# K and V of a cross attention in five matrix products instead of six, with a doubled half of the channels

## The reference, cut to what matters

```python
q = (query @ Wq + bq)                # 100 x 256 a batch
k = (key_value @ Wk + bk)            # 361 x 256 a batch, from 192 channels
v = (key_value @ Wv + bv)
attn = einsum(q, k) * scale          # 16 heads
attn = clip(attn, -CLAMP, CLAMP)     # CLAMP = 10000
attn = softmax(attn)
x = x + (attn @ v) @ Wo + bo
```

## Time and profile before

| | |
|---|---|
| median of 3 runs | 932.25 us (928.95 to 936.57) |
| the profiled execution, its own time | 938.05 us |
| span from first to last instruction in it | 936.2 us |
| granted TensorE clock, mean over the span | 0.909 |

### The profile page before, as it was taken

The page is one execution under the profiler, slowest core; times in us unless marked ns, Lnnn a source line. Parts: engine busy times, 40 slices in busy tenths (PEclk is TensorE's granted clock), DMA queues, the critical chain, the costliest instruction groups (busy, mean ns, idle before and its releaser), DMA issues.

```text
span 936.2 us, 21941 instructions
## 1 busy us (share of the span) xinstructions
PE 795.3 (85%) x8198; PEld 584.8 (62%) x8198; DVE 711.5 (76%) x1450; ACT 559.5 (60%) x1159; POOL 309.4 (33%) x254
## 2 busy tenths in 40 slices
PE   3788999999997786999789999997646999769995
PEld 2456666666665473778467777783214887459994
DVE  7779988888887796876656666745896988677866
ACT  6667667676664356443545556527897776663542
POOL 6235547555453433040512220003730221442400
PEclk9699999999999668899989999997556999889998
DMA  6433433434543447241465555455210000200002
GB/s 170 109 92 101 112 98 102 106 106 119 139 103 87 130 137 227 77 134 49 118 167 169 167 166 149 125 130 148 76 38 7 2 1 1 90 1 2 3 1 71
DMA packets 76935, 89.60 MB, mean 96 GB/s; under 512 B 22182, under 2 KB 64961, under 8 KB 76858
## 3 DMA queue, kind: packets, MB, share of 16 engines
q1 hardware_dynamic: 70026, 80.50, 31.0%
q0 software_dynamic: 6144, 7.42, 3.0%
q10 hardware_dynamic: 688, 0.66, 0.3%
HBM read 72.87 MB, written 15.43 MB: 94 GB/s over the span
## 4 chain that ended last, share of the span: by engine, by line
PE 44%; DVE 28%; issue 9%; ACT 7%; DMA 7%; POOL 4%; SPq 1%; DVEq 0%; ACTq 0%; POOLq 0%
PE ps L1217 11%; PE ps L1204 8%; DVE p L567 4%; PE ps L379 3%; DVE m L537 3%; PE ps L477 2%; PE ps L2239 2%; PE ps L551 2%; DVE m32c L500 2%; PE ps L532 2%; PE ps L579 2%; PE ps L2250 2%; DVE pmax L1691 1%; ACT area L2049 1%; DMA rden<-inverse 1%
## 5 line engine op out<-in xcount | busy, mean ns | idle before, releaser
L537 DVE TENSOR_REDUCE m<-ps 100x2 f32<-100x722 f32 x128 | 115.1, 899 | 41.1 <-PE ps L532 40.4
L558 ACT ACTIVATE p<-ps 128x800 f32<-128x800 f32 x128 | 106.8, 834 | 49.4 <-PE ps L551 47.4
L1266 ACT ACTIVATE hT<-ps,cols 128x500 f32<-128x500 f32 (+1 forms) x96 | 62.5, 651 | 103.3 <-PE ps L1204 103.1
L1273 DVE TENSOR_TENSOR hT_l<-hT,hT_h 128x500 f16<-128x500 f32 (+1 forms) x96 | 62.3, 652 | 61.2 <-ACT hT_h L1267 61.1
L1217 PE MATMUL ps<-w_h,hT_h 128*125 128x256 f16 (+1 forms) x384 | 105.6, 275 | 1.8 <-DVE x L1313 1.2
L567 DVE SCALAR_TENSOR_TENSOR p<-p 128x600 f32<-128x600 f32 x128 | 106.0, 830 | 0.0
L1217 PE MATMUL ps<-w_l,hT_h 128*125 128x256 f16 (+1 forms) x384 | 105.5, 275 | 0.0
L1217 PE MATMUL ps<-w_h,hT_l 128*125 128x256 f16 (+1 forms) x384 | 105.4, 274 | 0.0
L1109 POOL DMA_INDIRECT xe<-tokens,slot_of x32 | 43.1, 1346 | 156.3 <-PE ps L1227 106.4
L1204 PE MATMUL ps<-xe_h,w_h 128*128 128x500 f16 (+1 forms) x192 | 72.9, 380 | 19.7 <-ACT hT_h L1267 9.3
L1204 PE MATMUL ps<-xe_l,w_h 128*128 128x500 f16 (+1 forms) x192 | 72.5, 378 | 0.0
(11 more groups left out here) (347 smaller groups left out, 2132.6 us busy)
## 6 DMA issues: line engine op xcount, KB each, us to landing
sw<-in_L_ffn_w_dram SPq DMA_DIRECT2D x16, 512.0 KB, 6.1
sw<-in_L_ffn_w_dram SPq DMA_DIRECT2D x8, 1024.0 KB, 5.9
k_parts<-kp SPq DMA_DIRECT2D x32, 192.0 KB, 3.2
ks<-k_parts SPq DMA_DIRECT2D x32, 192.0 KB
stage<-in_L_xattn_W_f_dram SPq DMA_DIRECT2D x6, 1024.0 KB, 6.7
ctx_f<-in_ctxT_dram SPq DMA_DIRECT2D x16, 270.8 KB, 3.0
stage<-in_ctxT_dram SPq DMA_DIRECT2D x8, 541.5 KB, 8.6
area<-in_ctxT_dram SPq DMA_DIRECT2D x16, 270.8 KB, 6.0
```

Source lines behind the costliest of these rows:

```text
L537: v.tensor_reduce(m32[p][:, 2 * i:2 * i + 2], ps[0:T, at:at + 2, 0:KV], AX.X, ALU.max).then_inc(m_max, 1)
L558: s.activation(p32[:, i % HALF, :, :, :].rearrange("p j n t -> p n j t"), ps[:, t_bank(i):t_bank(i) + 2, 0:(KJ + 1) * T].rearrange("p n (j ...
L1266: s.activation(hT[:, f % 3, 0:m], bank[2 + f % 2][:, 0:m], ACT.Silu, bias=bias, scale=1.0 / WS)
L1273: v.tensor_tensor(hTp[p][1][:, f, 0:m], hT[:, f % 3, 0:m], hTp[p][0][:, f, 0:m], ALU.subtract).then_inc(f_l, 1)
```

## The change

1. The 192 channels are cut as 128 and 64 (`REST = 64`). The first 128 take three products as before. The other 64 are laid down twice, in partitions 0 to 63 and 64 to 127. `ctxh[p][:, 1, :]` holds their high part in the upper copy's place (0 to 63) and their low part in the other (64 to 127). One product with the doubled high weights gives high by high and low by high, a last one with 64 partitions gives the term with the low weights. So five products stand in place of six (`ctx_terms`). The low part of the doubled half is the raw value minus `ctx_rest`, which is zero in partitions 0 to 63.
2. `load_twice`: the context and the weights Wk and Wv come by three transfers each (128 partitions, 64, 64) in place of one.
3. `m_vector` is a `tensor_scalar` with two constants and one input; its output has a step of two elements.
4. In `a_tensor` at i=1, `pv_tensor` of the batch before now stands ahead of `v_tensor`.
5. In the loads of block 3 of the experts, `first_load` of the second half of expert 1's `w1` stands ahead of `second_load`.

```diff
-        m32c = sba("m32c", [T, H // 2])
+        m32c = sba("m32c", [T, H // 2, 2])[:, :, 0]
+        def load_twice(q, dst, src, done):
+            q.dma_start(dst[:, 0, :], src[0:128, :]).then_inc(done, 16)
+            for n in range(2):
+                q.dma_start(dst[n * REST:(n + 1) * REST, 1, :], src[128:CK, :]).then_inc(done, 16)
+
+        def ctx_terms(w, p):
+            hi, lo = w
+            return ((hi[:, 0, :], ctxh[p][:, 0, :]), (lo[:, 0, :], ctxh[p][:, 0, :]), (hi[:, 1, :], ctxh[p][:, 1, :]),
+                    (hi[:, 0, :], ctxl[p][:, :]), (lo[0:REST, 1, :], ctxh[p][0:REST, 1, :]))
@@ k_tensor
-            for k in range(2):
-                for i, j in TERMS:
-                    mm = pe.matmul(at[:, 0:KV], wk[i][:, k, c * 128:(c + 1) * 128], ctxp[p][j][:, k, :],
-                                   start=(n == 0), stop=(n == 5))
+            for n, (w, src) in enumerate(ctx_terms(wk, p)):
+                mm = pe.matmul(at[:, 0:KV], w[:, c * 128:(c + 1) * 128], src, start=(n == 0), stop=(n == 4))
@@ m_vector
-            v.scalar_tensor_tensor(m32c[:, :], m32[p][:, half * NP:(half + 1) * NP], CLAMP, least[:, :].broadcast_to((T, NP)), ALU.min,
-                                   ALU.max
+            v.tensor_scalar(m32c[:, :], m32[p][:, half * NP:(half + 1) * NP], CLAMP, -CLAMP, ALU.min, ALU.max
                                    ).then_inc(m_c, 1)
@@ c_scalar
+            of = slice(0, 128) if c == 0 else slice(REST, 128)
+            high = ctxh[p][:, 0, :] if c == 0 else ctx_rest[of, :]
+            s.activation(high, ctx_f32[p][of, c, :], ACT.Copy, accum_out=ctx_sum[of, c, bass.ds(b, 1)]).then_inc(c_h, 1)
@@ context_load
-            sp.dma_start(ctx_f32[p][:, :, :], ctx_d[b] if isinstance(b, int) else
-                         ctx_d[bass.ds(b, 1)].rearrange("o p c k -> (o p) c k")).then_inc(ctx_in[p], 16)
+            load_twice(sp, ctx_f32[p], ctx_rows[b], ctx_in[p])
@@ a_tensor
-                if i == 1 and has(b, 2):
-                    v_tensor(pe, b + 1, q, 0, (k_32, 2 * b + 5))
                 if i == 1:
                     pe.wait_ge(m_l, 2 * b + 2)
                 if i == 1 and from_(b, 1):
                     pv_tensor(pe, b - 1, q, NQ - 1)
+                if i == 1 and has(b, 2):
+                    v_tensor(pe, b + 1, q, 0, (k_32, 2 * b + 5))
@@ opening of SyncE; ScalarE's queue loads Wk and Wv by load_twice too
-            sp.dma_start(ctx_f32[0][:, :, :], ctx_d[0]).then_inc(ctx_in[0], 16)
+            context_load(sp, 0, 0)
-            sp.dma_start(ctx_f32[1][:, :, :], ctx_d[1]).then_inc(ctx_in[1], 16)
+            context_load(sp, 1, 1)
@@ loads (experts)
+                if is_shared(n):
+                    first_load(sp, e + 2, 1)
                 second_load(sp, e + 2)
-                first_load(sp, e + 2, 1)
+                if not is_shared(n):
+                    first_load(sp, e + 2, 1)
```

More of the change, by code:

```diff
@@ L149, in bias_row_tensor @@
         def bias_row_tensor(pe, part):
-            pe.wait_ge(wvo_in, 32)
+            pe.wait_ge(wvo_in, 64)
             for k in range(2 * part, 2 * part + 2):
@@ L243, in build @@
         w_in_ = {}
-        for name, rows_ in (("Wq", 128), ("Wk", KC), ("Wv", KC), ("Wo_heads", 128)):
+        for name, rows_ in (("Wq", 128), ("Wk", 128), ("Wv", 128), ("Wo_heads", 128)):
             k = HG if name == "Wo_heads" else 2
@@ L250, in build @@
         ctx_raw = sba("ctx_f32", [128, 2, 2, KV])
-        ctx_f32 = [ctx_raw[0:KC, p, :, :] for p in range(2)]
-        ctxp = [[sba(f"ctx{n}{p}", [KC, 2, KV], F16) for n in "hl"] for p in range(2)]
+        ctx_f32 = [ctx_raw[:, p, :, :] for p in range(2)]
+        ctxh = [sba(f"ctxh{p}", [128, 2, KV], F16) for p in range(2)]
+        ctxl = [sba(f"ctxl{p}", [128, KV], F16) for p in range(2)]
+        ctx_rest = sba("ctx_rest", [128, KV], F16)
         k32 = [sba(f"k32_{c}", [128, KV]) for c in range(CC)]
@@ L290, in build @@
         qk_sum = sba("qk_sum", [128, 4, B])
-        ctx_sum = sba("ctx_sum", [KC, 2, B])
+        ctx_sum = sba("ctx_sum", [128, 2, B])
         guard = sba("guard", [128, 4])
@@ L315, in build @@
         ctx_d = a["ctxT"].rearrange("(c p) (b k) -> b p c k", c=2, b=B)
+        ctx_rows = a["ctxT"].rearrange("c (b k) -> b c k", b=B)
+        REST = CK - 128
+        def load_twice(q, dst, src, done):
[6 more added lines that the diff above has]
+                    (hi[:, 0, :], ctxl[p][:, :]), (lo[0:REST, 1, :], ctxh[p][0:REST, 1, :]))
         TERMS = ((0, 0), (0, 1), (1, 0))
@@ L353, in split_weight @@
             else:
-                v.wait_ge(w_in[name], 16)
+                v.wait_ge(w_in[name], 48)
                 vs.inc(v.tensor_scalar(hi, src, WS, None, ALU.mult))
@@ L473, in v_tensor @@
             for j in ((0, 1), (2,))[u]:
[L474 to L480, removed]
+                for n, (w, src) in enumerate(ctx_terms(wv, p)):
+                    mm = pe.matmul(at[0:v_rows(j), j % 2 * C:(j % 2 + 1) * C], src[:, j * AT:j * AT + v_rows(j)], w,
+                                   start=(j != 1 and n == 0), stop=(n == 4), skip_group_check=True)
             mm.then_inc(v_mm, 1)
@@ L619, in y_tensor @@
             if is_first(b) and of[0] == 0:
-                pe.wait_ge(wvo_in, 48)
+                pe.wait_ge(wvo_in, 80)
             pe.wait_ge(o_n, b + 1)
@@ L644, in c_scalar @@
             if c == 0:
-                s.wait_ge(ctx_in[p], 16 * (t + 1))
+                s.wait_ge(ctx_in[p], 48 * (t + 1))
                 wait(s, v_mm, 2 * (b - 1))
-            s.activation(ctxp[p][0][:, c, :], ctx_f32[p][:, c, :], ACT.Copy,
-                         accum_out=ctx_sum[:, c, bass.ds(b, 1)]).then_inc(c_h, 1)
+            else:
+                wait(s, c_l, 2 * b)
+            of = slice(0, 128) if c == 0 else slice(REST, 128)
+            high = ctxh[p][:, 0, :] if c == 0 else ctx_rest[of, :]
+            s.activation(high, ctx_f32[p][of, c, :], ACT.Copy, accum_out=ctx_sum[of, c, bass.ds(b, 1)]).then_inc(c_h, 1)
         def c_gpsimd(g, b, p, c):
             g.wait_ge(c_h, 2 * b + c + 1)
-            g.tensor_tensor(ctxp[p][1][:, c, :], ctx_f32[p][:, c, :], ctxp[p][0][:, c, :], ALU.subtract).then_inc(c_l, 1)
+            high = ctxh[p][:, 0, :] if c == 0 else ctx_rest[:, :]
+            parts = ctxl[p][:, :] if c == 0 else ctxh[p][:, 1, :]
+            g.tensor_tensor(parts, ctx_f32[p][:, c, :], high, ALU.subtract).then_inc(c_l, 1)
         def context_load(sp, b, p):
             wait(sp, c_l, 2 * (b - 1))
-            sp.dma_start(ctx_f32[p][:, :, :], ctx_d[b] if isinstance(b, int) else
-                         ctx_d[bass.ds(b, 1)].rearrange("o p c k -> (o p) c k")).then_inc(ctx_in[p], 16)
+            load_twice(sp, ctx_f32[p], ctx_rows[b], ctx_in[p])
         def a_tensor(pe, b, t, p):
@@ L866, in guard_sums_tensor @@
                 for k in range(2):
+                    of = slice((0, REST)[k], 128)
                     mm = pe.matmul(UB_[row_:row_ + D, n // 4 * B:(n // 4 + 1) * B],
[L868 removed]
+                                   w_in_["Wv"][0][of, k, n * D:(n + 1) * D], ctx_sum[of, k, :],
                                    start=(n < 4 and k == 0), stop=(k == 1), skip_group_check=True)
@@ L2410, in _ @@
         def _(v):
+            v.memset(ctx_rest[0:REST, :], 0.0)
             vs.inc(v.memset(eps_col[:, :], LN_EPS))
-            v.memset(least[:, :], -CLAMP)
             v.memset(ks_flat[0][32:64, :].bitcast(F32), MINUS_ONES).then_inc(k_pad, 1)
@@ L2503, in _ @@
             for name in ("Wk", "Wq", "Wv"):
-                raw = w_in_[name][0]
-                s.dma_start(raw[:, :, :], a[f"L0_xattn_{name}"].rearrange("(k p) n -> p k n", k=raw.shape[1])
-                            ).then_inc(w_in[name], 16)
+                raw, src = w_in_[name][0], a[f"L0_xattn_{name}"]
+                if name == "Wq":
+                    s.dma_start(raw[:, :, :], src.rearrange("(k p) n -> p k n", k=2)).then_inc(w_in[name], 16)
+                else:
+                    load_twice(s, raw, src, w_in[name])
             s.wait_ge(vchain, 1)
@@ L2659, in _ @@
             k_store(sp, 1, 0, 1, 0)
-            sp.wait_ge(wvo_in, 16)
+            sp.wait_ge(wvo_in, 48)
             raw = w_in_["Wo_heads"][0]
```

3 lines of the change are left out of this document (removed).

## The result

The changed kernel takes 945.7 us (median of 4 runs, 945.4 to 948.0) against 932.1 of the kernel before, a ratio of 1.015 (1.012 to 1.018): slower, where 1.6% faster was forecast.

What follows compares the result with a forecast made beforehand. The order of work bounds it: a TensorE-VectorE chain, with a GpSimd-SyncE ring almost as long. -11.8 + 1.2 - 4.2 = -14.8 on the profiled 938.05 gives 923.25, or 917 us against the median; own range 908 to 924.

Steps and rivals of the forecast that it cites:

- the experts: Experts' loads: expert 1's second `w1` half issued earlier removes stalls of 6.32 and 2.59 us; gain 4.2, lower bound 2.6.
- the clamp: VectorE, maxima: 0.15 us without GpSimd's port; gains 0.52 at i=4 (with V's third group), 0.35 at i=0.
- K and V: TensorE, K and V products: a sixth of each group goes; 0.17 us for K, 0.25 and 0.12 for V.
- the 12 that the loop was to gain: Batches: 1.0 us in nine, 0.7 in the last four full ones, 11.8 in all; bounds 6 and 22.
- The transfers: SyncE's queue: context load issues three for one, 0.86 us more; no loss in a batch, 0.86 if cover goes.
- 1.1 of cover against 0.86: SyncE's queue: pauses ahead of `inv_store` and `q_store`, 1.1 us, hide the 0.86 of added context-load issues.
- the 0.4 and 0.35 of waiting: VectorE's waits for GpSimd: 0.4 us gained at i=4, a mean of 0.35 at i=0.
- The product ahead of V: TensorE: `pv_tensor` fills the idle before V, which waits for ScalarE's copy of K; 0.23 us on the path.
- The second ring: GpSimd and SyncE, from `q_store` through `inv_load` and back: 16.9 us, 1.2 slack; 1.0 of 1.7 gain taken.
- `qs<-mT`: TensorE's wait for the rows of maxima: if it appears instead, the ring of GpSimd and SyncE binds.
- The third case: Rival: the ring of GpSimd and SyncE holds the batch at 16.9 us, slack gained once; 928 us, chance 0.17.
- The opening: Before the loop: four more issues and a third more bytes delay the second context; +1.2 us, from 0 to +2.5.

Runs made afterwards that it cites:

- The version with both edits: Changed kernel with all K, V and guard-sum products over 128 rows and context loads behind the denominator load; 924.8 us (0.993) and 922.9 us (0.990).

## Why the prediction was wrong

Between the 917 of the forecast and the 945.7 measured lie 28 us. The version with both edits (922.9 and 924.8) has 20 to 23 of them back: they are the 64-row products and the queue. Of the 6 to 8 that stay, 4.2 would be the experts, whose gain the median does not show, and most of the rest the clamp; this split is an estimate.

**K and V: the step that failed.** The prediction put "one product costs by its columns and the rows are 96 or 128 alike (estimate)". For 96 and 128 that holds: with five products of 128 rows K takes 0.77 and V's two groups 1.10, even below the forecast 0.87 and 1.23 (which counted pauses in; K's saving is 0.16, 0.93 to 0.77, where 0.17 was forecast). But the fifth product has 64, which the change part of this document says and the sum did not cost. That gives back 0.21 in each K group and 0.41 in V's two, 1.05 us a batch with the third. Where the queue does not hide it, it costs 7 to 10 us, of the 12 that the loop was to gain; in the changed kernel as it stands, 5. The Trainium skill has the rule that speaks against this edit, and the prediction did not weigh it. "TensorEngine Tiling (Array Packing)" lists 64 rows as a tiling mode of its own beside 128 ("Available Configurations") and says under "Key Properties": "Changing tiling mode (not just tile) drains the TensorE". It does not say that a plain product over 64 rows sets such a mode. The trace agrees with that reading: the weight load of the 64-row product stands in the open, and the sorted guard sums show that the change costs and not the product. The page gives no price; here it is about 0.1 us a change. Whether it is this drain, and no other effect of the change, the runs do not tell.

**What the sum left out.** The guard sums use the same split. They stand outside the loop, and no term was written for them. They cost 7 us: 4.3 of their own, 1.2 more within batch 14, where the low clock stood behind them, and 1.5 that is not traced.

**The transfers: mis-sized.** "1.1 of cover against 0.86" was right for the kernel before (three transfers there: 1.002). In the changed kernel the two transfers of the doubled half take 0.59 us each to issue, not 0.43, and GpSimd has Q ready sooner. SyncE is late by itself then, and moving the loads gives back 7 us. By the prediction's own words that was 0.86 a batch "if that cover goes", 11 in 13 batches, but it put nothing in the sum. The prediction held the cover fixed while it shortened what makes the cover.

**The clamp: wrong.** It was to take 0.15 us. Alone in the kernel before it takes as much as the old one, and even the one in PSUM that always takes 0.25 brings nothing. So two steps failed: that a step of two keeps the instruction off GpSimd's port, and that the 0.4 and 0.35 of waiting were on the path. By the rule of the Trainium skill ("VectorE: DVE Perf Modes", "What auto-detection actually checks"), which names no step for f32, the clamp would still wait; the trace agrees, 158/841/1010 ns.

**The product ahead of V: right in direction.** 0.23 us a batch was forecast, 3.0 in 13 batches; 1 to 3.5 us were measured, about as much as the uncertainty.

**The second ring: right in kind.** It was named as the bound that lets only a part through, and with the rows as the sign (`qs<-mT` among TensorE's waits). It then grew by itself, which no case had. The third case (holds at 16.9) came nearest in mechanism, but its 928 lacks the K and V groups, the guard sums and the longer queue.

**The opening: right**, +1.6 against +1.2, within its range. A single opening varies by 2 to 4 us, so one pair could have been luck; but on average it ends at 48.3 in the six kernels with the old loads (47.2 to 49.4) and at 49.8 in the eleven with the new ones (48.1 to 51.9), +1.5.

**The experts: wrong in size.** The stall of 6.32 us was a real row, of one execution. The page could not show that it varies: 7.3, 6.4, 2.9, 2.2 and none in five others. Its removal is worth at most 2.6 us of the median (the lower end of 0.997 to 1.001), and nothing that could be seen. The profiled execution lay 5.8 us above the median, and a part of it was this stall. The prediction took the 5.8 off and the stall too, and so counted it twice.

## What to carry to other kernels

Before a contraction is cut unevenly, look at the number of rows of each product next to its neighbours': a filled-up 128-row product can be cheaper than a 64-row one between two of 128. Follow a changed layout into everything that reads it, also outside the loop. A gap in a queue is cover only as long as the engine that makes it stays as late as it was. And a stall that occurs once in a profile is worth its length only if the execution's own time is near the median.

## What the runs showed of the hardware

- A change between 128 and 64 rows from one product to the next cost TensorE about 0.1 us in the K and V groups (361 and 256 columns) and 0.07 in the guard sums (16 columns). The latter took 0.70 us sorted and 5.08 in turn.
- A TENSOR_SCALAR of 100x8 f32 in SBUF with a step of two in its output took 158 to 1010 ns beside GpSimd's work, where the old form with two inputs took 153 to 1004; one of 8x100 in PSUM took 248 ns all 32 times.
- It stays open why two issues with 64 partitions take 0.59 us where those with 48 take 0.43. Periods of about 18 us in single batches, also in the fastest version (in one, `q_store` took 2.46 us to issue in place of 0.9), were not traced to a cause.
